# Second expert matrices kept in SBUF, and padded low halves of the attention keys written by GpSimd

## What is computed

```python
x = x + L0_xattn(norm(x), ctx)   # linear attention
x = x + L0_ffn(norm(x))          # 8 decision trees of depth 7
x = x + L1_xattn(norm(x), ctx)   # 16 heads, masked softmax, no output matrix
x = x + L1_ffn(norm(x))          # ternary weights, depthwise convolution
x = x + L2_xattn(norm(x), ctx)   # 16 heads, output matrix and biases
x = x + L2_ffn(norm(x))          # gated, four ternary 256/1024 layers
x = x + L3_xattn(norm(x), ctx)   # 32 heads of 8 columns, output matrix
x = x + L3_ffn(norm(x))          # 8 experts, top 1
```

```python
probs = softmax(x_flat @ Wg + bg); e = argmax(probs)
h = gelu(x @ W1[e] + b1[e])                  # 256 x 256
out = probs[e] * (h @ W2[e] + b2[e])         # 256 x 256
```

## Time and profile before

| what | value |
|---|---|
| median of 3 runs | 1650.95 us |
| the profiled execution | 1653.79 us |
| its span, first to last instruction | 1651.9 us |
| mean granted TensorE clock | 0.947 of full speed |
| first attention (L1X) | about 318 to 490 us |
| second attention (L2X) | about 600 to 866 us, its start beside the layer before |
| third attention (L3X) | about 1220 to 1543 us |
| job loop | 1565 to 1652 us |

### The profile page before, as it was taken

How to read it: one execution, slowest core, us unless ns; L and a number is a source line. 1 busy time by engine, 2 the same in 40 slices (tenths; PEclk the granted TensorE clock), 3 DMA queues, 4 the chain that set the end, 5 groups by cost and what they waited for, 6 DMA issues and landing times.

```text
span 1651.9 us, 26234 instructions
## 1 busy us (share of the span) xinstructions
PE 1439.7 (87%) x9842; PEld 1075.5 (65%) x9849; DVE 1073.0 (65%) x2358; ACT 757.3 (46%) x1264; POOL 116.4 (7%) x168
## 2 busy tenths in 40 slices
PE   7999999778878995799888999999988899989356
PEld 5666666557773443477776878787854777779245
DVE  4465665778877873787746464645458988876234
ACT  2212111267773674575752222222234877788123
POOL 1000000000000000111000000000011101010413
PEclk9999999999998997999989999999999999999679
DMA  9552201410000000000009810000100000000176
GB/s 323 185 180 77 77 15 62 168 41 14 13 3 1 1 1 7 18 14 13 2 2 339 261 53 1 1 1 0 33 7 7 1 7 2 7 2 2 64 258 225
DMA packets 60269, 102.64 MB, mean 62 GB/s; under 512 B 11076, under 2 KB 48957, under 8 KB 59967
## 3 DMA queue, kind: packets, MB, share of 16 engines
q1 hardware_dynamic: 57726, 84.53, 15.6%
q10 hardware_dynamic: 544, 12.16, 2.2%
q0 software_dynamic: 1872, 4.27, 0.7%
HBM read 79.24 MB, written 39.40 MB: 72 GB/s over the span
## 4 chain that ended last, share of the span: by engine, by line
PE 51%; issue 18%; DVE 15%; ACT 5%; DVEq 4%; DMA 3%; SPq 1%; POOL 1%; ACTq 1%; POOLq 1%
PE bank L1989 9%; PE bank L1990 9%; PE bank L1681 7%; PE bank L1659 7%; DVE MB L913 3%; PE bank L1786 2%; DVE plo L931 2%; DMA jx<-copy_routed 2%; PE bank L1837 2%; PE bank L1587 1%; PE bank L1790 1%; PE bank L1791 1%; PE bank L1757 1%; PE bank L1759 1%; PE bank L1719 1%
## 5 line engine op out<-in xcount | busy, mean ns | idle before, releaser
L931 DVE TENSOR_TENSOR plo<-e,phi 120x512 f16<-120x512 f32 x256 | 180.2, 709 | 51.1 <-ACT phi L1411 47.4
L1405 ACT ACTIVATE e<-bank 120x512 f32<-120x512 f32 x256 | 150.9, 589 | 43.8 <-PE bank L1791 34.7
L1411 ACT ACTIVATE phi<-e 120x512 f16<-120x512 f32 x256 | 161.7, 632 | 8.7
L913 DVE TENSOR_REDUCE MB<-bank 128x4 bf16<-128x480 f32 x256 | 156.0, 649 | 13.8 <-PE bank L1759 10.6
L1336 ACT ACTIVATE act<-bank,bin 127x512 f32<-127x512 f32 x64 | 43.2, 688 | 167.2 <-DVE dec L751 163.2
L1659 PE MATMUL bank<-xT,winT 128*127 128x512 f32 (+1 forms) x256 | 114.6, 593 | 1.3 <-ACTq L1307 1.3
L1681 PE MATMUL bank<-woutT,msk 128*128 128x256 f32 (+1 forms) x512 | 115.2, 379 | 0.0
L670 DVE TENSOR_SCALAR high<-raw 128x512 int32<-128x512 int32 x96 | 41.0, 427 | 111.8 <-ACT raw L1540 60.8
L1681 PEld LDWEIGHTS bank<-woutT,msk 128*128 128x128 f32 (+1 forms) x512 | 96.9, 190 | 15.4
L1989 PE MATMUL bank<-hah,h1w 128*128 128x512 f32 x256 | 101.3, 396 | 3.6 <-DVE hal L673 3.6
L550 POOL TENSOR_TENSOR veps<-mv,ceps 128x4 f32<-128x4 f32 x32 | 8.9, 277 | 1346.1 <-DVEq L641 1214.2
(11 more groups left out here) (308 smaller groups left out, 3525.7 us busy)
## 6 DMA issues: line engine op xcount, KB each, us to landing
copy_routed<-zeros SPq DMA_DIRECT2D x1, 17028.0 KB
jw<-copy_experts SPq DMA_DIRECT2D x23, 641.0 KB, 5.1
seen<-in_h1T SPq DMA_DIRECT2D x8, 512.0 KB, 6.9
seen<-in_h2T SPq DMA_DIRECT2D x8, 512.0 KB, 5.1
h1w<-copy_h1T SPq DMA_DIRECT2D x1, 4096.0 KB, 17.1
h2w<-copy_h2T SPq DMA_DIRECT2D x1, 4096.0 KB, 14.2
ctxp<-in_ctxT SPq DMA_DIRECT2D x13, 240.0 KB, 2.9
jx<-copy_routed SPq DMA_DIRECT2D x23, 132.0 KB, 4.9
```

The source lines that it names most:

```text
L913: dve.tensor_reduce(MB[:, t, h0 // 8, SK + h0 % 8:SK + h0 % 8 + 4], b[:, 0:4 * SK].rearrange("p (h k) -> p h k", h=4), AX.X, ALU.max).then ...
L931: dve.tensor_tensor(plo[:, g % 3, :], e32[:, g % 3, :], phi[:, g % 3, :], ALU.subtract).then_inc(s.lo, 1)
L1405: act.activation(e32[:, g % 3, :], bank[2 + g % 3][0:SK, :], ACT.Exp).then_inc(s.exp, 1)
L1411: act.activation(phi[:, g % 3, :], e32[:, g % 3, :], ACT.Copy).then_inc(s.phi, 1)
```

## The change

1. The second matrices of all 8 experts (`w2e`) are loaded once into SBUF (`experts`, 128 x 8 x 2 x 256 float32) by two DMAs that SP issues when the scores of the third pair of L3X are done; they lie where the even pairs' padded keys were. PE reads each job's expert number into a register (`job_expert`, behind `job_transposes(j)`) and takes the matrix from there. The kits lose the columns W2: 770 columns, 385 KB. Two of the staging DMAs go.
2. The first kits are no longer issued together: SP issues kit 0, waits for the scatter, issues the rows of job 0, then kit and rows of each further job in turn.
3. `low_keys` leaves ACT for GpSimd, as `tensor_scalar` with multiply in place of an activation; for each pair of an attention it stands ahead of the bias add and of the norm's steps.

```diff
@@ -38,7 +38,7 @@
...
 OH = (NT - TT - 1, 2 * (NT - TT) - 1 + TT - 1)
-W1, W2, B1, B2, KIT = 0, K2 * D, 2 * K2 * D, 2 * K2 * D + K2, 2 * K2 * D + K2 + D
+W1, B1, B2, KIT = 0, K2 * D, K2 * D + K2, K2 * D + K2 + D
@@ -318,7 +318,9 @@
...
     jtok = put("jtok", [128, NO], I32, at)
-    assert at[0] <= r5
+    assert at[0] <= kpad_at
+    at = [kpad_at]
+    experts = put("experts", [128, NE, K2, D], F32, at)
@@ -357,6 +359,7 @@
...
         sem("h_" + n) for n in ("consts", "zeroed", "sent", "norm", "xt", "xT", "up", "act", "down", "out"))
+    ld_experts = sem("ld_experts")
     ld_job = [sem(f"ld_job{b}") for b in range(NB)]
@@ -391,7 +394,7 @@
...
     W_COPIED = 5 * 16
-    ZEROED = (1 + 2 * K2 + 2) * 16
+    ZEROED = (1 + K2 + 2) * 16
     LD_L2, LD_L3X, LD_L3 = (4 + 3 + 2 * 2 + 2) * 16, 4 * 16, 2 * 16
@@ -496,12 +499,16 @@
...
                              zeros[:].unsqueeze(1).broadcast_to([128, SLOTS // 128, CELL])).then_inc(Hf.zeroed, 16)
-                for c, w in ((W1, "w1e"), (W2, "w2e")):
-                    for k in range(K2):
-                        sp.dma_start(kits[:, :, c + k * D:c + (k + 1) * D], a[w][:, k * 128:(k + 1) * 128, :]).then_inc(Hf.zeroed, 16)
+                for k in range(K2):
+                    sp.dma_start(kits[:, :, W1 + k * D:W1 + (k + 1) * D], a["w1e"][:, k * 128:(k + 1) * 128, :]).then_inc(Hf.zeroed, 16)
                 sp.dma_start(kits[:, :, B1:B1 + K2], a["b1e"].rearrange("p (e k) -> e p k", e=NE)).then_inc(Hf.zeroed, 16)
...
+        l3 = X[L3X.name]
+        sp.wait_ge(l3.sc, L3X.u0 + (PAIRS - 1) * L3X.units)
+        for k in range(K2):
+            sp.dma_start(experts[:, :, k, :], a["w2e"][:, k * 128:(k + 1) * 128, :].rearrange("e p n -> p e n")).then_inc(ld_experts, 16)
+
         def job_weights(j, e):
@@ -510,18 +517,17 @@
...
         sp.wait_ge(Hf.tab, 1)
-        for j in range(NB):
-            job_weights(j, sp.value_load(jtab[0:1, 1, j:j + 1], min_val=0, max_val=NE - 1))
-        sp.wait_ge(Hf.sent, 16 * NT)
         for j in range(JOBS):
...
                 sp.wait_ge(Hf.out, j - NB + 1)
-                job_weights(j, sp.value_load(jtab[0:1, 1, j:j + 1], min_val=0, max_val=NE - 1))
+            job_weights(j, sp.value_load(jtab[0:1, 1, j:j + 1], min_val=0, max_val=NE - 1))
+            if j == 0:
+                sp.wait_ge(Hf.sent, 16 * NT)
             job_rows(j, sp.value_load(jtab[0:1, 0, j:j + 1], min_val=0, max_val=NE * PLACES))
...
                             (ld_l1, LD_L1), (ld_l2, LD_L2), (mask_ready, (0, 16 * 5, 16 * 9)[sum(phases > q for q in (2, 4))]),
-                            (w_copied, W_COPIED), (ld_h1, PAIRS * LD_SEEN + 64), (ld_h2, 16 if phases > 5 else 0), 
+                            (w_copied, W_COPIED), (ld_h1, PAIRS * LD_SEEN + 64), (ld_h2, 16 if phases > 5 else 0), (ld_experts, K2 * 16),
                             (ld_l3x, LD_L3X if phases > 6 else 0), (ld_l3, LD_L3 if phases > 6 else 0),
@@ -568,8 +574,17 @@
...
+        def low_keys(L, j):
+            l, K, rm = X[L.name], Kpad[L.name], rm4 if L.hg == 4 else rm8
+            pool.wait_ge(l.kpad, L.c0 + j + 1)
+            for r in range(L.hg):
+                last = pool.tensor_scalar(K[j % 2][:, 1, r, :, :], klo[:], rm[:, r:r + 1], None, ALU.mult)
+            last.then_inc(l.klow, 1)
+
         for p in range(6):
             for i in range(PAIRS):
+                if p in (2, 4):
+                    low_keys(L1X if p == 2 else L2X, i)
                 if p == 4:
@@ -600,6 +615,7 @@
...
         for i in range(PAIRS):
+            low_keys(L3X, i)
             add_bias(6, i)
@@ -1385,13 +1401,6 @@
...
-            def low_keys(j, r):
-                if r == 0:
-                    act.wait_ge(s.kpad, L.c0 + j + 1)
-                last = act.activation(K[j % 2][:, 1, r, :, :], klo[:], ACT.Copy, scale=rm[:, r:r + 1])
-                if r == L.hg - 1:
-                    last.then_inc(s.klow, 1)
-
             def maxima_rows(j, t):
@@ -1424,8 +1433,6 @@
...
                     high_queries(i + 1, u - 1)
-                if ahead and u in L.lows:
-                    low_keys(i + 1, L.lows.index(u))
                 if ahead and u in L.flipped:
@@ -2076,6 +2083,10 @@
...
+        def job_expert(j):
+            e = pe.value_load(jtab[0:1, 1, j:j + 1], min_val=0, max_val=NE - 1)
+            return experts[:, ds(e, 1), :, :].rearrange("p o w n -> p (o w) n")
+
         def job_up(j):
@@ -2086,12 +2097,12 @@
...
-        def job_down(j):
+        def job_down(j, w):
             pe.wait_ge(Hf.act, j + 1)
...
             for k in range(K2):
-                last = pe.matmul(bank[6 + j % 2][:, 0:D], jh[:, j % 3, k, :], jw[:, j % NB, W2 + k * D:W2 + (k + 1) * D], start=(k == 0),
+                last = pe.matmul(bank[6 + j % 2][:, 0:D], jh[:, j % 3, k, :], w[:, k, :], start=(k == 0),
                                  stop=(k == K2 - 1))
@@ -2102,13 +2113,17 @@
...
             pe.matmul(bank[0][0:1, 0:NE], onesb[:, 0:1], acc[:, len(ROUTES), :], start=True, stop=True).then_inc(Hf.cnt, 1)
+            pe.wait_ge(ld_experts, K2 * 16)
+            pe.wait_ge(Hf.tab, 1)
+            weights = []
             for j in range(JOBS + 2):
...
                     job_transposes(j)
+                    weights.append(job_expert(j))
                 if 1 <= j <= JOBS:
...
                 if j >= 2:
-                    job_down(j - 2)
+                    job_down(j - 2, weights[j - 2])
```

## The result

The changed kernel takes **1660.15 us** (median of 7 runs, 1658.17 to 1660.88), the kernel before 1650.95 us (median of the 7 runs beside them). The ratio is 1.0055, 95% interval 1.0041 to 1.0069: slower by 9 us, where 4 us faster was forecast. The profiled execution of the changed kernel has a span of 1658.7 us.

The account below looks back on a forecast made before the run. VectorE was taken to pace the first and third attentions, DMA bytes with the loop's chain the jobs; -5.7 - 6.2 + 8.5 - 1 = -4.4 from 1650.95 gave 1646.5 us, range 1633 to 1664.

Parts of the forecast that it names:

- start of the jobs: Start of the job loop: first rows go out behind one kit instead of six, first output earlier, -5.7 us.
- pace of the jobs: Job loop: smaller kits cut the 22 output intervals from 2.63 to 2.35 us, -6.2 us.
- the copies beside VectorE: Attentions: GpSimd's copies, taken as 1.05 us each, collide with VectorE instructions at 0.45 us per collision, +8.5 us.
- the moved bias adds: Attentions: bias adds behind the copies cost about +4, stalls removed at their old places give -5, net -1 us.
- ScalarE's relief: Attentions: ScalarE loses 64 instructions, 69 us, but TensorE waits for VectorE there; priced at 0, other end -6 us.
- The bias adds move too: Attentions: six bias adds behind copies each stretch one VectorE instruction, 1.2 us; with old stalls gone, net -1 us.
- The end: Job loop behind the attentions: earlier start of the jobs, -5.7 us, and faster pace, -6.2 us.
- The slow rival: Attentions, units 3 to 9 behind new keys: GpSimd's copies hold VectorE up, +35 us, 1673 us in all; chance 0.18.
- My own mark for being wrong: Wrong if job output intervals stay above 2.55 us, or the attentions together grow by over 15 us or shrink.

Follow-up runs that it names:

- e3: Changed kernel with each bias add put ahead of GpSimd's four or eight copies again, nothing else: 1649.73 us.
- e1: Changed kernel with the padded low halves of the keys back on ScalarE, so only the resident second matrices are left of the change: 1639.09 us.
- e7: Changed kernel with each GpSimd copy replaced by a memset of the same size to zero, bias add still behind: 1650.61 us.
- e9: Changed kernel with the low halves written by ScalarE again, GpSimd keeping only its wait for the padded keys ahead of the bias add: 1644.15 us.
- e2: Kernel before the change with the padded low halves written by GpSimd, expert weights as before: 1670.79 us.
- e4: Changed kernel with GpSimd's copies for the last two pairs of each attention cut to 8 elements, waits and order kept: 1656.5 us.
- e8: Changed kernel with GpSimd's copies in the first attention alone; ScalarE writes the low halves in the two others: 1644.95 us.
- e12: Changed kernel with each bias add ahead of GpSimd's key work and each copy replaced by a same-size memset to zero: 1642.21 us.
- e6: Resident matrices alone (low halves on ScalarE), second matrix taken at a fixed address, so TensorE loads no register in the jobs: 1640.97 us.

## Why the prediction was wrong

Term by term, in us; the measured ones from the ratios and, for the two of the end, from the profiles:

```
term                        forecast (ends)      measured
start of the jobs           -5.7 (-3, -7)        -6.2
pace of the jobs            -6.2 (-0.7, -9.5)    -7.0
the copies beside VectorE   +8.5 (0, +35)        +10.7   (e3 against e1, with any relief in it)
the moved bias adds         -1   (-5, +8)        +10.9   (changed kernel against e3)
ScalarE's relief             0   (-6)              -     (not measured apart)
sum                         -4.4                 +9.1
```

(The four measured terms add to +8.4; the rest is within their intervals.)

- **The step that failed is "The bias adds move too"**: put at -1 us, measured +10.9. I saw that they fall behind the copies and priced each at one stretched instruction of 1.2 us, paid back by the stalls removed from their old places. Two things are wrong in it. The old places were cheap: I took the one bad row at the third attention's head for the others, while at 725.61 the add stretches one subtraction and delays TensorE little. And the new place is not "somewhere beside VectorE" but behind the padded keys, where VectorE next casts the values: 2.42 us instead of 0.29, with plo queued behind it and TensorE behind plo (4.3 us instead of 2.0, in two pairs). The wait was in my text ("the bias only when the next pair is projected"), but I asked only whether it is late for its reader, not whom it would then meet. This meeting is worth 4.6 of the 10.9 us. The others, which e7 and e9 show without it (7.3 and 5.7), I had no term for: they come with a lower granted clock, and their cause stays open.
- **The copies** came out near the forecast (+10.7 for +8.5) in part by luck, since errors both ways offset each other. One copy takes 2.7 us, not 1.05; my lower bound of 0.95 was right for a memset (0.90) and not for a multiply by a scalar of each partition. A collision, however, does not last for the whole copy. Of two copies, the first began at 1373.12 and the second at 1376.28. The subtraction at 1376.40 takes 1.48 us; the one at 1374.89, in the middle of the first copy, keeps its 0.68:

```profile
1373.12 5.84 POOL L581 TENSOR_SCALAR Kpad_even<-klo,rm 128x960 f16<-128x960 f16 x2
```

```profile
1374.89 0.68 DVE L947 TENSOR_TENSOR plo<-e,phi 120x512 f16<-120x512 f32 x1
1375.83 0.66 DVE L929 TENSOR_REDUCE MB<-bank 128x4 bf16<-128x480 f32 x1 [0.26 <-PE bank L1766]
1376.40 1.48 DVE L947 TENSOR_TENSOR plo<-e,phi 120x512 f16<-120x512 f32 x1
```

  The Trainium skill (SBUF — State Buffer, Who interferes with whom) says that the second of the two fully blocks for the other's whole instruction. The trace disagrees for these copies: at most 0.8 us lost of 2.7. It agrees for the bias add, where the cast ended 0.15 us behind the add. So plo grew by 6 us in all, not 13.5, but the price was passed on in full or more, in part through TensorE's clock: over the whole kernel its busy time grew by 13 us with no matmul more. Nor does the second attention pass on a tenth, as I took it: the largest loss lies there. And the copies that prepare an attention's first pair, which I left out, cost as well: from 640 to 690 us the offset to the kernel before grows by 1.7 to 1.9 us in the changed kernel, e2, e3 and e4, and by 0.2 us or less in e1, e7, e8, e9 and e12, which have no copy there.
- **The end** was right in both terms, and in its mechanisms: kits out of the way of the first rows, smaller transfers that land sooner. TensorE is the engine that is nearly full now, and its waits for rows are down to 0.5 us. That the pace came out at 2.36 us a job against 2.35 forecast is in part luck: I got there by adding a register load, and e6 shows no cost of it beyond the noise. What else lifts TensorE's 1.98 us a job was not tried. The Trainium skill (SBUF — State Buffer, The DMA setup-cost knee) would have had 4.4 for the pace, and it was 7.0; the rows' landing fell from 4.9 to 3.5 us at the same size, which its fit by size alone does not give.
- **The slow rival** was right in sign and in its place in the attentions, wrong in mechanism: it took 35 us from copies that block throughout. My own mark for being wrong, attentions longer by over 15 us, was met: they grew by 19.3 us from the start of the first to the last projected residual.
- **ScalarE's relief** at 0 fits what the runs show, though none isolates it: TensorE's waits for ScalarE in the attentions stayed at 9.8 and 9.4 us. So the GpSimd part had little to win.

## What to carry to other kernels

When work is inserted into an in-order queue, follow what stands behind it: its new start time, and then what the neighbours are doing at that time. Here half of the loss came with an untouched instruction that ran some 25 us later and, in two pairs, met casts with plo and TensorE queued behind them; putting it ahead of the new work took 10 us back. Before moving work off an engine, look whether anything waits for that engine: TensorE's few waits for ScalarE did not shrink, so no gain shows from the 63 us taken off it, and the best version of all keeps them there.

## What the runs showed of the hardware

- One operation on three engines, 128x960 f16 times a scalar of each partition: VectorE 0.47 us, ScalarE 1.08, GpSimd 2.7. GpSimd's with 8 elements takes 0.34 us (eight in 2.69), so the rest goes by elements, 2.5 ns each; its memset of 960 takes 0.90 us. A memset is no measure for a copy.

```profile
1358.63 2.69 POOL L584 TENSOR_SCALAR Kpad_even<-klo,rm 128x8 f16<-128x8 f16 x8 [27.53 <-DVEq L911]
```

- Who gets through when VectorE's subtraction (two inputs in SBUF, 0.68 us alone) meets a copy (2.68 us alone). The changed kernel's trace has 55 overlaps of the two. A subtraction that starts 0.1 to 1.0 us behind a copy's start takes 0.74 to 1.48 us (14 cases); ten of them end 1.60 us behind that start, the four others 1.8 to 1.9. One that starts later keeps its 0.68. One that starts up to 0.25 us ahead of the copy, or within 0.04 us behind its start, keeps 0.68 too, and the copy takes 3.0 to 3.2. The casts of the values (0.29 us alone) have another pattern. Three that start 0.2, 0.4 and 0.9 us behind a copy's start end 1.2 us behind it. Those that start 1.1 to 1.7 us behind it keep their time. The five that start 1.8 or 2.3 us behind it are held until 0.15 us behind the copy's end: below, a copy from 360.10 to 362.80 and two casts, the second held to 362.94, together 1.27 us instead of 0.49.

```profile
360.10 2.70 POOL L581 TENSOR_SCALAR Kpad_odd<-klo,rm 128x960 f16<-128x960 f16 x1
361.67 1.27 DVE L938 CAST V_odd<-v 120x256 f16<-120x256 f32 x2
```

  Why some are let through and others are not was not tried. The bias add holds both back to its end: the twelve stretched subtractions that meet it in the kernel before, the changed kernel and e3 end 0.55 us behind it, the changed kernel's two casts 0.15 us.
- TensorE's granted clock gives the same 489 matmuls 42.2 or 45.5 us of busy time in two kernels that do not differ there.
